# Attention and ternary feed-forward block: the Hadamard rotation folded into channel halves, and the orders of work laid out anew

## The reference, cut to what matters

```python
x = x + layernorm(attention(layernorm(x), ...))      # 16 heads of 16, latent k and v of 64
x = x + layernorm(ffn(layernorm(x), weight))
```

```python
xh = x @ H                                  # H: 256x256 Hadamard matrix / 16
scale = max(max|xh| over channels, 1e-5) / 7
xq = clip(round(xh / scale), -8, 7) * scale
wq = ternary(weight) * mean|row|
y = xq @ wq.T
```

## Time and profile before

| | |
|---|---|
| Median of the runs | 1477.69 us |
| The profiled execution's own time | 1477.54 us, span 1475.7 us |
| PE, weight load, DVE, ACT, POOL busy | 93%, 41%, 79%, 79%, 50% of the span |
| Opening, before the first scores | 43 us |
| Equal rounds | 29 of 42.83 us, from 128.4 to 1370.5 us |
| After the last scores of the last batch | from 1399 to 1476 us, PE mostly idle |
| Granted PE clock | full in the equal rounds, 0.56 over the last 56 us |
| DMA | 241 MB, busy share of the 16 engines some 57% in the rounds |

### The profile page before, as it was taken

The page is one execution under the profiler, slowest core; times in us unless marked ns, Lnnn a source line. Parts: engine busy times, 40 slices in busy tenths (PEclk is TensorE's granted clock), DMA queues, the critical chain, the costliest instruction groups (busy, mean ns, idle before and its releaser), DMA issues.

```text
span 1475.7 us, 35923 instructions
## 1 busy us (share of the span) xinstructions
PE 1369.4 (93%) x12330; PEld 597.9 (41%) x12330; DVE 1165.8 (79%) x2732; ACT 1158.9 (79%) x1252; POOL 732.3 (50%) x1060
## 2 busy tenths in 40 slices
PE   5889999999999999999999999999999999999842
PEld 3334444444444444444444444434444344444321
DVE  5767888888888888888888888888888888888642
ACT  0677888888888888888888888888888888888912
POOL 2324554554455455545555654555565455544333
PEclk9999999999999999999999999999999999999965
DMA  5455566556555655555566555556655655565210
GB/s 178 143 166 151 158 184 202 161 169 188 158 153 182 201 171 170 175 169 151 178 196 182 163 171 179 151 176 187 191 156 169 189 150 173 183 201 154 82 53 30
DMA packets 174541, 241.45 MB, mean 164 GB/s; under 512 B 28320, under 2 KB 145184, under 8 KB 174496
## 3 DMA queue, kind: packets, MB, share of 16 engines
q1 hardware_dynamic: 140160, 206.78, 46.5%
q10 hardware_dynamic: 34336, 34.08, 7.4%
HBM read 154.80 MB, written 69.21 MB: 152 GB/s over the span
## 4 chain that ended last, share of the span: by engine, by line
PE 62%; DVE 15%; POOL 12%; issue 6%; ACT 2%; DMA 1%; SPq 0%; DVEq 0%; POOLq 0%
PE heads_ps L644 23%; PE scores_ps L631 12%; PE misc_ps L565 8%; PE misc_ps L533 5%; PE misc_ps L584 4%; POOL y_sb L955 4%; DVE diagonal L1163 3%; DVE x L1101 3%; PE misc_ps L544 3%; DVE ln_stats L1021 3%; PE misc_ps L574 2%; DVE xT L1041 2%; PE misc_ps L555 2%; POOL ln_root L929 2%; POOL ln_rstd L929 2%
## 5 line engine op out<-in xcount | busy, mean ns | idle before, releaser
L839 ACT ACTIVATE probs<-scores_ps 128x1024 f32<-128x1024 f32 x768 | 762.0, 1024 | 222.1 <-PE scores_ps L631 217.0
L644 PE MATMUL heads_ps<-probs,v_sb 128*32 128x512 f32 x4096 | 531.7, 603 | 4.3 <-ACT probs L846 2.8
L1163 DVE TENSOR_TENSOR diagonal<-scores_ps,comp 128x1024 f32<-128x1024 f32 x256 | 309.6, 1209 | 101.1 <-PE scores_ps L631 101.1
L631 PE MATMUL scores_ps<-q_rep,k_rep 64*128 64x128 f16 (+2 forms) x5120 | 346.9, 251 | 33.5 <-DVE diagonal L1163 22.8
L631 PEld LDWEIGHTS scores_ps<-q_rep,k_rep 64*128 64x128 f16 x5120 | 167.1, 94 | 418.9 <-ACT probs L839 161.6
L846 ACT ACTIVATE probs<-diagonal 128x2048 f32<-128x2048 f32 x128 | 245.1, 1915 | 0.0
L922 POOL TENSOR_TENSOR ln_neg_mean<-zero,ln_moments 128x4 f32<-128x4 f32 x128 | 26.3, 206 | 363.1 <-DVE ln_moments L1029 362.5
L1075 DVE SCALAR_TENSOR_TENSOR weighted<-misc_ps,edges 128x384 f32<-128x384 f32 x256 | 129.1, 546 | 64.8 <-PE misc_ps L533 35.6
L964 POOL TENSOR_TENSOR k_hl<-weighted,k_hl 128x768 f16<-128x768 f32 x64 | 105.8, 1653 | 117.4 <-DVE k_hl L1082 117.4
L969 POOL TENSOR_TENSOR heads_c<-heads_c,den_spread 128x1024 f32<-128x1024 f32 x32 | 75.8, 2369 | 163.7 <-DMA den_spread<-den_scratch 163.7
L644 PEld LDWEIGHTS heads_ps<-probs,v_sb 128*32 128x32 f32 x4096 | 87.6, 108 | 169.4 <-issue 164.0
(11 more groups left out here) (110 smaller groups left out, 1476.5 us busy)
## 6 DMA issues: line engine op xcount, KB each, us to landing
q_rep<-q_scratch SPq DMA_DIRECT2D x128, 384.0 KB, 4.1
k_rep<-k_scratch SPq DMA_DIRECT2D x256, 192.0 KB, 3.6
q_scratch<-q_hl SPq DMA_DIRECT2D x64, 384.0 KB, 2.3
k_scratch<-k_hl SPq DMA_DIRECT2D x64, 384.0 KB, 3.7
x_in<-in_L_attn_x_dram ACTq DMA_DIRECT2D x32, 512.0 KB, 4.3
heads_c<-heads SPq DMA_DIRECT2D x256, 64.0 KB, 2.4
x_res<-in_L_attn_x_dram ACTq DMA_DIRECT2D x32, 512.0 KB, 4.0
den_spread<-den_scratch SPq DMA_DIRECT2D x256, 64.0 KB, 3.4
```

The costliest lines, as they stand in the source:

```text
L631: ins = mm(scores_ps[:, place + par, at:at + n * P], k_rep[rows, pair, kv_, k_cols], q_rep[rows, pair, qv_, q_cols], start=True, stop=True)
L644: ins = mm(heads_ps[W32 * g:W32 * (g + 1), :], v_sb[:, b.slot, kt, at:at + W32], probs[:, quad % 2, g, kt, :], start=(kt == 0), stop=(kt = ...
L839: nc.scalar.activation(flat[:, :, at:at + S], scores_ps[:, place:place + 2, :], ACT.Exp, scale=EXP_SCALE).then_inc(off_probs, 1)
L1163: v.tensor_tensor(diagonal[:, quad % 2, 2 * two:2 * two + 2, :], scores_ps[:, place:place + 2, :], comp[:].rearrange("p t n -> p (t n)").u ...
```

## The change

POOL forms, from x1 before it is normalised, the sum and the difference of the two channel halves into x1n, in two operations of 128x512. rstd(3) also forms the doubled negated mean, with a wait for it. The apply then is two operations of 128 channels for each of the four token tiles: the sum gets the doubled mean and the factor, the difference only the factor. The matrix is the one of 128, the first block of the old one, and each matmul of `xh` writes 128 columns; the two channel halves no longer add up, so each pair of 16-bit halves is a group of its own. All five orders are other ones. The bank table follows from PE's order: `lat` and the first `q` change places.

```diff
--- before.py
+++ after.py
@@ -65,29 +65,28 @@
 STEPS = 32
 
 TENSOR_STEPS = {
-    0: [("z", 0, 0)], 1: [("z", 1, 0), ("pv_end", 3, 0)], 3: [("xT", 0, 0), ("pv_end", 3, 1)], 5: [("xT", 1, 0), ("pv_end", 3, 2)],
-    7: [("lat", 0, 0)], 8: [("q", 0, 0), ("pv_end", 3, 3)], 10: [("q", 0, 1), ("pv", 0, 0)], 12: [("x1T", 0, 0), ("x1T", 1, 0)],
-    13: [("pv", 0, 1)], 14: [("k", 0, 0)], 15: [("pv", 0, 2), ("k", 1, 0)], 17: [("pv", 0, 3), ("v", 0, 0), ("xh", 0, 0)],
-    19: [("xh", 1, 0), ("pv", 1, 0)], 21: [("pv", 1, 1), ("pv", 1, 2)], 22: [("pv", 1, 3)],
-    24: [("q", 1, 0), ("q", 1, 1), ("y", 0, 0), ("y", 0, 1)], 26: [("pv", 2, 0), ("qintT", 0, 0)], 28: [("y", 1, 0), ("y", 1, 1)],
-    30: [("pv", 2, 1)], 31: [("pv", 2, 2), ("pv", 2, 3)],
+    0: [("z", 0, 0), ("z", 1, 0)], 1: [("xT", 0, 0), ("xT", 1, 0)], 2: [("pv_end", 3, 0)], 3: [("pv_end", 3, 1)],
+    5: [("pv_end", 3, 2), ("pv_end", 3, 3)], 7: [("q", 0, 0), ("lat", 0, 0)], 9: [("q", 0, 1)], 10: [("pv", 0, 0)],
+    12: [("x1T", 0, 0), ("x1T", 1, 0), ("pv", 0, 1)], 14: [("k", 0, 0), ("pv", 0, 2)], 15: [("k", 1, 0), ("pv", 0, 3)],
+    17: [("v", 0, 0), ("xh", 0, 0)], 19: [("xh", 1, 0), ("pv", 1, 0)], 21: [("pv", 1, 1), ("pv", 1, 2)], 23: [("pv", 1, 3)],
+    24: [("q", 1, 0), ("y", 0, 0), ("q", 1, 1), ("y", 0, 1)], 26: [("pv", 2, 0), ("qintT", 0, 0)], 28: [("y", 1, 0), ("y", 1, 1)],
+    30: [("pv", 2, 1), ("pv", 2, 2), ("pv", 2, 3)],
 }
 SCALAR_STEPS = {
-    6: [("load_res", 0)], 8: [("z_apply", 0)], 11: [("z_apply", 1)], 12: [("x1T", 0)], 13: [("x1T", 1)], 15: [("z_apply", 2)],
-    18: [("z_apply", 3), ("load_x", 0)], 20: [("round_x", 0)], 21: [("round_x", 1)], 22: [("round_x", 2)], 23: [("round_x", 3)],
-    27: [("qintT", 0)],
+    5: [("load_res", 0)], 6: [("z_apply", 0), ("z_apply", 1)], 13: [("load_x", 0), ("x1T", 0), ("x1T", 1), ("z_apply", 2)],
+    20: [("z_apply", 3)], 22: [("round_x", 0), ("round_x", 1)], 23: [("round_x", 2), ("round_x", 3)], 29: [("qintT", 0)],
 }
 VECTOR_STEPS = {
-    0: [("z", 0)], 1: [("z", 1), ("x1_make",)], 2: [("xT", 0)], 3: [("z_stats",)],
-    4: [("xT", 1), ("z_moments",), ("x1_stats",), ("lat", 0)], 6: [("x1_moments",)], 9: [("heads_end", 3)], 11: [("q_split", 0)],
-    12: [("x1_low", 0)], 13: [("x1_low", 1), ("k_split", 0), ("den_invert",), ("k_split", 1)], 16: [("v", 0), ("heads", 0)],
-    18: [("act_scales",)], 23: [("v", 1), ("x_stats",), ("heads", 1), ("x_moments",)], 24: [("quantize",), ("q_split", 1)],
-    30: [("y", 0), ("y", 1), ("y_stats",), ("y_moments",), ("heads", 2)],
+    0: [("z", 0), ("z", 1), ("z_stats",), ("z_moments",), ("x1_make",)],
+    7: [("xT", 0), ("xT", 1), ("x1_stats",), ("x1_moments",), ("heads_end", 3)], 9: [("lat", 0)], 10: [("q_split", 0)],
+    13: [("x1_low", 0), ("x1_low", 1), ("den_invert",), ("k_split", 0)], 15: [("k_split", 1)], 18: [("v", 0)],
+    19: [("heads", 0), ("act_scales",)], 21: [("v", 1)], 22: [("heads", 1)], 26: [("quantize",)], 27: [("x_stats",), ("q_split", 1)],
+    30: [("y", 0), ("y", 1), ("x_moments",), ("y_stats",), ("y_moments",), ("heads", 2)],
 }
-POOL_STEPS = ["rstd4", "x1_apply", ("q", 0), ("k", 0), ("k", 1), "heads_normalize", "x_apply", "add_out", ("q", 1), "rstd2"]
-SYNC_STEPS = [("own", "spread", 1), ("a", "gather_den"), ("a", "pack_den"), ("pre", "store_q", 0), ("a", "compact", 1),
-              ("a", "return_den"), ("a", "spread_den"), ("pre", "store_k", 1), ("pre", "store_k", 0), ("pre", "spread", 0),
-              ("c", "store_out"), ("pre", "store_q", 1), ("own", "compact", 0)]
+POOL_STEPS = ["rstd4", "x1_apply", ("q", 0), ("k", 0), "heads_normalize", "add_out", ("k", 1), ("q", 1), "x_apply", "rstd2"]
+SYNC_STEPS = [("own", "spread", 1), ("a", "gather_den"), ("a", "compact", 1), ("a", "pack_den"), ("pre", "store_q", 0),
+              ("a", "return_den"), ("pre", "store_k", 0), ("a", "spread_den"), ("pre", "spread", 0), ("pre", "store_q", 1),
+              ("c", "store_out"), ("pre", "store_k", 1), ("own", "compact", 0)]
 
 ORDER_ALL = [step for h in sorted(TENSOR_STEPS) for step in TENSOR_STEPS[h] if step[0] in PARTS]
 
@@ -201,7 +200,7 @@
         w_up_v = sb("w_up_v", [P, D])
         ident = sb("ident", [P, P])
         ident_bf = sb("ident_bf", [P, P], BF16)
-        hadamard = sb("hadamard", [P, DC, D], F16)
+        hadamard = sb("hadamard", [P, P], F16)
 
         edges = sb("edges", [P, 2, EDGE])
         comp = sb("comp", [P, T, P])
@@ -249,7 +248,7 @@
 
         ln = {n: dict(stats=sb(f"ln{n}_stats", [P, T, 2, 3]), moments=sb(f"ln{n}_moments", [P, T, 2]), var=sb(f"ln{n}_var", [P, T]),
                       var_eps=sb(f"ln{n}_var_eps", [P, T]), root=sb(f"ln{n}_root", [P, T]), rstd=sb(f"ln{n}_rstd", [P, T]),
-                      neg_mean=sb(f"ln{n}_neg_mean", [P, T]), shift=sb(f"ln{n}_shift", [P, T]))
+                      neg_mean=sb(f"ln{n}_neg_mean", [P, T]), neg_mean_twice=sb(f"ln{n}_neg_mean_twice", [P, T]), shift=sb(f"ln{n}_shift", [P, T]))
               for n in (1, 2, 3, 4)}
 
 
@@ -313,8 +312,8 @@
 
         def part_count(stage, b, part):
             return PARTS[stage] * (b.made if GROUP[stage] == "pre" else b.number) + part + 1
-        xn_ready, high_done, split_done, x1_high, x1_ready, x1n_ready = map(sem, (
-            "xn_ready", "high_done", "split_done", "x1_high", "x1_ready", "x1n_ready"))
+        xn_ready, high_done, split_done, x1_high, x1_ready, x1_folded, x1n_ready = map(sem, (
+            "xn_ready", "high_done", "split_done", "x1_high", "x1_ready", "x1_folded", "x1n_ready"))
         absmax_ready, xscale_ready, inv_ready, qint_ready, ffn_normed, out_ready = map(sem, (
             "absmax_ready", "xscale_ready", "inv_ready", "qint_ready", "ffn_normed", "out_ready"))
         z_var_scaled, z_rstd, z_shift, square_ready, ws_steps, g_max_raw = map(sem, (
@@ -377,7 +376,7 @@
             rest = [
                 (decay, c_decay), (fall_head, c_decay[0:1, (T - 1) * P:T * P].to_broadcast([P, P])),
                 *[(wo[64 * half:64 * half + 64], Wo.rearrange("(half c r) n -> half r c n", half=2, c=DC)[half]) for half in range(2)],
-                (hadamard[:], c_hadamard), (headmask[:], c_headmask),
+                (hadamard[:], c_hadamard[:, 0, 0:P]), (headmask[:], c_headmask),
             ]
             for dst, src in first:
                 sp.dma_start(dst, src).then_inc(first_loaded, 16)
@@ -581,8 +580,8 @@
                     t = 2 * part + n
                     for c in range(DC):
                         for hl in range(2):
-                            ins = mm(tokens(bank)[:, n, :], x1_hl[:, hl, c, t * P:(t + 1) * P], hadamard[:, c, :],
-                                     start=(c == 0 and hl == 0), stop=(c == DC - 1 and hl == 1))
+                            ins = mm(tokens(bank)[:, n, c * P:(c + 1) * P], x1_hl[:, hl, c, t * P:(t + 1) * P], hadamard[:],
+                                     start=(hl == 0), stop=(hl == 1))
                 ins.then_inc(in_psum["xh"], 1)
 
             def qintT_stage(b, part, piece):
@@ -936,6 +935,10 @@
                     nc.gpsimd.tensor_tensor(m["var_eps"][:], m["neg_mean"][:], m["rstd"][:], ALU.mult).then_inc(z_shift, 1)
                     pool.wait_ge(z_shift, b.number + 1)
                     nc.gpsimd.tensor_tensor(m["shift"][:], m["var_eps"][:], y_shift[:, b.slot, :], ALU.add).then_inc(ln_ready[n], 1)
+                elif n == 3:
+                    nc.gpsimd.tensor_tensor(m["neg_mean_twice"][:], m["neg_mean"][:], m["neg_mean"][:], ALU.add).then_inc(ln_ready[n], 1)
+                    pool.wait_ge(ln_ready[n], b.number + 1)
+                    nc.gpsimd.tensor_tensor(m["shift"][:], m["neg_mean_twice"][:], m["rstd"][:], ALU.mult)
                 else:
                     shift = y_shift[:, b.slot, :] if n == 2 else m["shift"][:]
                     nc.gpsimd.tensor_tensor(shift, m["neg_mean"][:], m["rstd"][:], ALU.mult).then_inc(ln_ready[n], 1)
@@ -950,10 +953,16 @@
 
             def x1_apply(b):
                 m = ln[3]
+                left, right = x1[:, b.slot, :, 0:P], x1[:, b.slot, :, P:D]
+                pool.wait_ge(x1_ready, b.number + 1)
+                nc.gpsimd.tensor_tensor(x1n[:, :, 0:P], left, right, ALU.add)
+                nc.gpsimd.tensor_tensor(x1n[:, :, P:D], left, right, ALU.subtract).then_inc(x1_folded, 1)
+                pool.wait_ge(x1_folded, b.number + 1)
                 rstd(3, b)
                 for t in range(T):
-                    ins = nc.gpsimd.tensor_scalar(x1n[:, t, :], x1[:, b.slot, t, :], m["neg_mean"][:, t:t + 1], m["rstd"][:, t:t + 1],
-                                                  ALU.add, ALU.mult)
+                    nc.gpsimd.tensor_scalar(x1n[:, t, 0:P], x1n[:, t, 0:P], m["neg_mean_twice"][:, t:t + 1], m["rstd"][:, t:t + 1],
+                                            ALU.add, ALU.mult)
+                    ins = nc.gpsimd.tensor_scalar(x1n[:, t, P:D], x1n[:, t, P:D], m["rstd"][:, t:t + 1], None, ALU.mult)
                 ins.then_inc(x1n_ready, 1)
 
```

## The result

The changed kernel takes 1538.01 us (median of 4 runs, 1533.56 to 1540.17) against 1477.45 us (1475.47 to 1477.95) for the kernel before in the same session: ratio 1.0409, 95% interval 1.0389 to 1.0429. It is 60.6 us slower; I had forecast 21 us faster, and my range ended at 1475. The profiled execution took 1537.0 us, with a span of 1535.2 and a mean granted clock of 0.959 (0.975 in the profiled execution of before).

The account below looks back on a forecast made before the run. PE was taken to bound the kernel. Work of 40.2 us and waits of 1.9 made a round of 42.1 against 42.83; 0.73 less x 29 = 21.2 us, so 1456.3 us, range 1440 to 1475.

Parts of the forecast that it names:

- POOL's apply and the doubled mean: POOL's normalisation of x1: eight operations at 2.5 us (2.2 to 3.0) against 2.16, plus 0.27 us for the doubled mean.
- time 0: Origin of the forecast's times within a round: the end of the second pv of quad 2 on PE.
- PE's arrival at x1T: PE at the turning of x1n at 14.35 us, x1n there at 15.1: a wait of 0.75 us (0.2 to 1.4).
- Cover of the folds: POOL's two sum and difference operations, 2.4 us, end some 0.8 us before x1's moments arrive, so cost nothing.
- The start of the round: DVE's new sequence: x1's moments out at 10.6 us, last heads 11.2; PE's 0.70 us diagonal wait becomes 0.35.
- The narrow matmuls: Rotation on PE with 128 columns a matmul: two groups a round, 0.86 us less work, nothing saved at worst.
- The denominators: SP's queue, DVE and POOL up to heads_normalize: den_packed lands in 1.7 us, PE waits 0.7 us at y (0 to 2.3).
- y waiting for the denominators: Rival: spread_den behind store_k 0 comes late and PE waits at y; 1480 to 1503 us, taken at 1485, chance 0.17.
- Contention at quantize: Rival: DVE's quantize waits for a whole POOL operation of 2.36 us, PE held 0.6 us; 1474 us, chance 0.17.
- The ends: Kernel outside the equal rounds: savings at half clock against POOL's longer chain, taken at zero, -3 to +3 us.
- The sum of a round: PE's work of 40.2 us plus waits of 1.9 us: a round of 42.1 us against 42.83.
- groups that now stand together: PE's groups of z, xT and pv placed next to each other: 0.35 us less work a round.

Follow-up runs that it names:

- forms run: The kernel before with seven forms of POOL operation, four of each, added behind the end of its work to time them; its own total time says nothing.
- one_diff: The changed kernel with the difference half normalised by one wide POOL operation, factor broadcast, in place of four; 1505.2 us, ratio 1.0189 to the kernel before.
- load_late: New orders with the old rotation, the load of x moved back from step 13 to 18 of ACT's order; 1512.4 us, ratio 1.0259 to the kernel before.
- pack_first: New orders with the old rotation, pack_den and store_q 0 put back ahead of compact 1 in SP's order; 1473.2 us, ratio 0.9979.
- new_best: The changed kernel with pack_den ahead of compact 1, doubled mean formed earlier, unused shift left out, difference half first in one operation; 1462.4 us, ratio 0.9908.
- math_only: The kernel before with its old orders and the new rotation, folds and eight POOL operations included; 1664.7 us, ratio 1.1281.
- orders_only: The kernel before with the five new orders and the old rotation, no folds, four POOL operations; 1514.0 us, ratio 1.0254.
- new_both: The changed kernel with the difference half in one POOL operation and pack_den back ahead of compact 1 in SP's order; 1483.3 us, ratio 1.0049.

## Why the prediction was wrong, step by step

**The step that failed** is *POOL's apply and the doubled mean*. I set eight operations of 128 elements at 2.5 us, between 2.2 and 3.0; they take 4.36. The bounds were built from one row of another shape, as if a length were all that changed, and the row I had did not bear on the second form at all: an operation with one step instead of two. The forms run has it at 0.59 us against 0.43, and the eight together at 4.08. Nearly all of that 1.86 us lies on the path: without it x1n would have been there 15.27 us after time 0, just before PE at 15.37 (next paragraph). one_diff, which takes 1.3 us off the apply and changes nothing else, gives back 32.8 us. rstd3, priced at 1.95, took 1.97.

**PE's arrival at x1T.** I had PE at 14.35 and x1n at 15.1 us after time 0, a wait of 0.75. Measured from the same point (612.65): PE at 15.37, x1n at 17.13, the wait 1.82. The 1.0 of PE holds 0.44 for ACT before step 12, of which I only said that a part of the wait may be ACT's. Without it the wait for POOL would have been longer by as much. I had seen load_res wait for x1_make, and taken it at none, 0 to 0.2 us; ACT stands idle for 1.19 us there.

**Cover of the folds.** The folds took 2.5 us, as priced (2.4), but ended at 10.72, not at 9.75: z's moments came 0.2 later, and rstd4 took 3.2 us instead of 2.5, its first operations 0.32 to 0.44 us instead of 0.20, beside DVE's x1_make. So the cover of 0.8 was gone, and they end 0.1 behind the moments of x1. I had named x1_make beside rstd4 under contention, and then priced only quantize.

**The start of the round** was right: moments of x1 out at 10.63 (10.6), the last heads at 11.2 (11.2), the diagonal's wait gone from 22.8 us to 2.9.

**The narrow matmuls** were priced at 0.86 us and give 0.56 over the run. The row was read rightly, and its distance to the next start (0.55) would have given the same 0.86; what was wrong is that it stood for the narrow rotation, behind which the next group starts 0.14 us later. The 0.66 us that I had worked out from the Trainium skill's figure was nearer to what came, but not by its rule: the pairs start 57 ns apart and not 81.

**The denominators** were half right. Pack's issue was foreseen to 0.1 us (compact ends at 16.3, measured 628.92 - 612.65 = 16.27), the landing was not: 3.3 us instead of 1.7, since I had moved x's load in the sum of ACT's queue only and never laid it beside den_packed. With pack_den moved back ahead the changed kernel gains at most 5 us, the new orders alone 41. My rival, y waiting for the denominators, occurred, among the equal rounds, in two early ones alone, those of 44.6 us, and cost 1.5 us: of the 10.6 us that PE waits for heads_c in 4 places 9.7 are one, at the end. In the round shown heads_c ends at 646.35 and y starts at 646.96. The rival had the right chain with the wrong place: the wait that chain makes falls on den_invert and k, not on y, and only load_late moved it to y.

**Contention at quantize** was seen and doesn't bind. It lasts 1.54 us in the median and up to 2.76, where 0.68 was usual:

```profile
L1144 DVE TENSOR_SCALAR x_hl<-ffn x32: 682/1535/2762, 158.4 to 1517.2; 128x1024 bf16<-128x1024 f32 x32
```

In the round above it lasts from 647.54 to 649.24 and begins inside add_out (646.31 to 648.68); it ends 0.56 us after add_out, about its own undisturbed length. This agrees with the Trainium skill, "SBUF — State Buffer", section Who interferes with whom, by which a DVE operation in a two-port mode and one of GpSimd exclude each other for a whole instruction; that quantize runs in such a mode is taken from its length and not shown. But PE's wait for it (L592) shows only at the end of the kernel, 3.9 us once, as before.

**The lower clock** was in neither the sum nor a rival. I had a full clock in all 29 rounds and priced waits by their own length. In the changed kernel the waits carry another 13 us with them.

**The ends** I took at zero, -3 to +3; they cost +15.2 (5.5 + 11.3 - 1.6). There POOL's chain stands bare: the longest wait at x1T is 16.1 us, 12.9 before.

**The sum of a round.** An undisturbed round was to be 42.1 and is 43.9. The waits were to be 1.9 us and are 2.26 (1.82 and 0.44); the forecast ones for the diagonal, for heads and for y (0.35, 0.1, 0.7) didn't come, or hardly. The rest, work and small gaps, was to be 40.2 and is 43.88 - 2.26 = 41.6. Of these 1.4 us the narrow matmuls are 0.3. Another 0.6 are the small gaps between rows: I had taken them out of the 41.4 as if they were waits that the sum carries elsewhere, and it doesn't. And the 0.35 for groups that now stand together shows nowhere: before, a round without its two waits is 42.83 - 0.83 = 42.0, and in pack_first, which has the new orders and the old rotation, it is 42.5 - 0.45 = 42.05. Some 0.15 us stay unexplained. That new_best has 42.05, as forecast for the change, is therefore partly luck: its waits are 0.45 us and not 1.9.

The reading that PE sets the round and the rest counts where PE waits stood; the chances did not, as 1.86 us of POOL's time was off with a bound of 0.5 behind it.

## What to carry to other kernels

An operation split in two, or given another form, has to be priced by a row of that very form, or with a bound as wide as the engine's fixed cost; on an engine that the bound engine already waits for, that one price decides the sign. Price a group by the distance to the next start, and from the same form in the same place: two rows of 0.62 us stood for 0.55 and 0.69 us here. Gaps that are taken out of the work have to come back in the sum. When a transfer is small and its consumer stands in front of others in its engine's order, look at what large load is issued just before it, and when two costs lie one behind the other on the same engine, take away both before judging either: here one was worth 33 us alone, the other 5, and both 55.

## What the runs showed that I had not expected

- GpSimd's tensor_scalar with one step is slower than with two: 0.59 us against 0.43 at 128 elements, 0.905 against 0.54 at 256. A tensor_tensor with a factor spread over 128x512 takes 1.04 us, less than half of four one-step operations of 128x128 (2.35).
- How long PE had waited before the granted clock fell to the lower level differs. In the changed kernel it fell behind 12 of the first 30 waits at x1T, of 1.8 to 2.1 us each (most with 0.44 or 0.46 for ACT close before); in math_only behind every wait of 4.6 to 5.0 us, and behind one of 1.78; in orders_only behind one wait of 1.68 us at k, and behind none of 1.56 or less; in one_diff and new_both behind none of 0.6 to 0.7 in the rounds. Why one round of the changed kernel has it and the next, with the same waits, hasn't, stays open.
- A DMA of 32 KB lands after 1.7 us in the kernel before, 1.9 behind four of 64 KB, and 3.1 to 3.3 when 512 KB were issued on another queue up to 1.6 us before it.
